# Float32 projections replaced by three float32r products of high and low parts, in the front of an attention and channel-mixing kernel

## The reference

```python
def attn(x):                       # 16 heads of 16 channels
    q, k, v = (heads(x @ W.T + b) for W, b in ((Wq, bq), (Wk, bk), (Wv, bv)))
    attn = softmax(einsum('bhnd,bhmd->bhnm', q, k) * 4.0)
    return concat(einsum('bhnm,bhmd->bhnd', attn, v)) @ Wo.T + bo
def mix(x):
    xr, xk = mu_r * x + (1 - mu_r) * x_prev, mu_k * x + (1 - mu_k) * x_prev
    return sigmoid(xr @ W_r.T) * (relu(xk @ W_k.T) ** 2 @ W_v.T)
x = x + attn(layernorm(x))
x = x + mix(layernorm(x))
```

## Time and profile before

| | us |
|---|---|
| median of three runs | 2742.4 |
| profiled execution | 2745.94 |
| its span, first to last instruction | 2744.2 |
| mean granted TensorE clock (share of full) | 0.999 |
| TensorE, VectorE, ScalarE, GpSimd busy | 2719.2, 2484.4, 2494.8, 373.5 |

### The profile page before, as it was taken

The page is one execution under the profiler, slowest core; times in us unless marked ns, Lnnn a source line. Parts: engine busy times, 40 slices in busy tenths (PEclk is TensorE's granted clock), DMA queues, the critical chain, the costliest instruction groups (busy, mean ns, idle before and its releaser), DMA issues.

```text
span 2744.2 us, 57924 instructions
## 1 busy us (share of the span) xinstructions
PE 2719.2 (99%) x22619; PEld 904.0 (33%) x22619; DVE 2484.4 (91%) x4853; ACT 2494.8 (91%) x2800; POOL 373.5 (14%) x752
## 2 busy tenths in 40 slices
PE   9999999999999999999999999999999999999999
PEld 6552222222222222222222222222222222224776
DVE  6659999999999999999999999999999999985774
ACT  7779999999999999999999999999999999987555
POOL 7761000000000000000000000000000000103451
PEclk9999999999999999999999999999999999999999
DMA  6642010100000000000010101010101000212541
GB/s 198 214 156 59 12 35 12 28 19 21 21 23 24 23 23 24 23 23 24 17 30 10 33 12 34 12 35 12 34 13 45 24 22 20 60 41 79 167 131 47
DMA packets 145363, 126.30 MB, mean 46 GB/s; under 512 B 59969, under 2 KB 127425, under 8 KB 145089
## 3 DMA queue, kind: packets, MB, share of 16 engines
q1 hardware_dynamic: 145088, 122.59, 14.9%
HBM read 72.75 MB, written 47.19 MB: 44 GB/s over the span
## 4 chain that ended last, share of the span: by engine, by line
PE 85%; SPq 9%; DMA 2%; DVE 2%; issue 1%; ACT 1%; POOL 0%; POOLq 0%; ACTq 0%
PE psum L1359 34%; PE psum L1255 17%; PE psum L1327 16%; PE psum L1389 4%; PE psum L1907 3%; SPq L153 3%; SPq L158 3%; PE psum L1270 3%; PE psum L1404 2%; PE psum L447 2%; PE psum L1895 2%; SPq L126 2%; DMA a_qs<-q_parts 2%; SPq L127 2%; DVE a_mx L1033 1%
## 5 line engine op out<-in xcount | busy, mean ns | idle before, releaser
L1033 DVE TENSOR_REDUCE a_mx<-psum 128x1 f32<-128x512 f32 x3096 | 1930.0, 683 | 118.3 <-PE psum L1327 98.9
L1255 PE MATMUL psum<-a_qs,a_ks 50*128 50x512 f16 x4096 | 804.7, 384 | 3.6 <-DMA a_qs<-a_mrows 2.4
L1327 PE MATMUL psum<-a_ks,a_qs 48*128 48x512 f16 x3596 | 759.9, 382 | 12.5 <-DVE a_mx L1033 2.2
L955 ACT ACTIVATE m_gate<-psum 128x1024 f32<-128x1024 f32 x684 | 676.7, 1028 | 29.5 <-PE psum L1255 17.8
L955 ACT ACTIVATE m_y<-psum 128x1024 f32<-128x1024 f32 x682 | 675.0, 1028 | 28.8 <-PE psum L1255 16.9
L955 ACT ACTIVATE p_x<-psum 128x1024 f32<-128x1024 f32 x682 | 674.7, 1028 | 28.9 <-PE psum L1255 17.4
L1255 PEld LDWEIGHTS psum<-a_qs,a_ks 50*128 50x128 f16 x4096 | 193.8, 93 | 677.2 <-ACT m_y L955 166.5
L1359 PE MATMUL psum<-m_gate,a_vst 128*32 128x256 f32 (+1 forms) x4248 | 406.3, 454 | 0.0
L1359 PE MATMUL psum<-p_x,a_vst 128*32 128x256 f32 (+1 forms) x4232 | 403.4, 453 | 0.0
L1359 PE MATMUL psum<-m_y,a_vst 128*32 128x256 f32 (+1 forms) x4224 | 403.2, 453 | 0.0
L1327 PEld LDWEIGHTS psum<-a_ks,a_qs 48*128 48x128 f16 x3596 | 205.7, 93 | 405.9 <-DVE a_mx L1033 328.4
(11 more groups left out here) (147 smaller groups left out, 1605.8 us busy)
## 6 DMA issues: line engine op xcount, KB each, us to landing
m_x<-x SPq DMA_DIRECT2D x24, 512.0 KB, 5.7
a_qs<-q_parts SPq DMA_DIRECT2D x384, 32.0 KB, 2.2
sums<-a_o SPq DMA_DIRECT2D x256, 34.0 KB
q_parts<-m_split SPq DMA_DIRECT2D x16, 512.0 KB, 3.5
v_rows<-m_v SPq DMA_DIRECT2D x16, 512.0 KB, 2.8
k_parts<-m_split SPq DMA_DIRECT2D x16, 512.0 KB, 3.9
a_ks<-k_parts SPq DMA_DIRECT2D x64, 128.0 KB
a_vin<-v_rows SPq DMA_DIRECT2D x64, 128.0 KB, 6.0
```

Source lines behind the costliest of these rows:

```text
L955: ac.activation(p_sb[n % WEIGHTS][:, 2 * pair:2 * pair + 2, :], psum[:, at:at + 2, :], ACT.Exp, scale=SCALE).then_inc(s_exp, 1)
L1033: dve.tensor_reduce(peak, psum[:, bank(at), :], AX.X, ALU.max).then_inc(s_mx, 1)
L1255: mm = te.matmul(psum[:, pair_of_banks(u) + par, :], ks[row:row + MR, (it // QB) % 2, pair, c * P:(c + 1) * P], qs[row:row + MR, it % QRIN ...
L1327: te.matmul(psum[:, bank(slot(n, par)), :], qs[row:row + SR, pit % QRING, at:at + P], keys, start=True, stop=True).then_inc(s_sp, 1)
```

## The change

From block 1 on, q, k and v are computed from parts. ScalarE's copy of the transposed block and of each weight matrix into a float32r tile keeps the high part (`x_high`, `w_high`); VectorE subtracts it from the source to get the low part (`x_low` by `lows`, `w_low` by `weights_low`). Each float32 matmul becomes three float32r matmuls: high by high, low weight by high x, high weight by low x. So a job has six matmuls in place of two, a value half twelve in place of four. Block 0 keeps its float32 matmuls. `turned(blk + 1)` moves ahead of `value(blk, 0)`, and on ScalarE `keep_turned` ahead of `keep_v(blk, 0)`. `turned` waits for `lows` of the block before; `project(blk, 0)` waits for `lows` of its own block ahead of its last two matmuls. `lows(1)` stands before `whole_norm(1)`; `lows(2)`, and each later even one, stands behind the second Newton round; the odd ones stand between two groups of maxima.

The unit rows: GpSimd fills one 32x2048 piece at the start (`set_unit`), and three DMAs on SyncE's queue copy its two rows to the other seven places (`copy_units`, after the loads of x for blocks 2 and 3); the four 32x4096 fills inside the front go, and so does `first_k`'s wait for them.

The attention runs `even(0)`, `odd(1)` first and `sixteen` from period 2 on. The weights' and x parts' tiles are allocated in memory that the last stage's tiles use later. The diff, cut:

```diff
+class FrontBuffers:
+
+
+    def __init__(self, ctx, nc):
+        def sb(name, shape, dt=F32):
+            return ctx.enter_context(nc.sbuf_tensor(name, shape, dt))
+
+        self.w = {n: sb(f"p_w{n}", [P, KH, C]) for n in "qkv"}
+        self.w_high = {n: sb(f"p_wh{n}", [P, KH, C], F32R) for n in "qkv"}
+        self.w_low = {n: sb(f"p_wl{n}", [P, KH, C], F32R) for n in "qkv"}
+        self.w_sq = sb("p_wsq", [P, 2, KH, C])
+        self.x_high, self.x_low = ([sb(f"p_x{n}{s}", [P, KH, TB], F32R) for s in range(2)] for n in "hl")
+
...
-    def set_unit(self, pool, buf, par):
-
-        pool.memset(self.ks[par * HALF + 32:par * HALF + 64, buf, :, :], SHIFT_UNIT).then_inc(self.s_unit, 1)
-        pool.wait_ge(self.s_unit, 2 * buf + par + 1)
+    def set_unit(self, pool):
+
+        pool.memset(self.ks[32:64, 0, 0, :], SHIFT_UNIT).then_inc(self.s_unit, 1)
+
+    UNITS_INC = 3 * DMA
+
+    def copy_units(self, sp):
+
+        sp.wait_ge(self.s_unit, 1)
+        rows = self.ks[SR:MR, 0, 0, :]
+        other = slice(HALF + SR, HALF + MR)
+        sp.dma_start(self.ks[SR:MR, 0, 1, :], rows).then_inc(self.s_units, DMA)
+        sp.dma_start(self.ks[SR:MR, 1, :, :], rows.unsqueeze(1).to_broadcast([PARTS, GP, N])).then_inc(self.s_units, DMA)
+        sp.dma_start(self.ks[other, :, :, :].rearrange("p b u n -> p (b u) n"),
+                     rows.unsqueeze(1).to_broadcast([PARTS, 2 * GP, N])).then_inc(self.s_units, DMA)
 
...
     def first_k(self, sp, n):
-        if n == 0:
-            sp.wait_ge(self.s_unit, 2)
-        else:
+        if n:
             sp.wait_ge(self.s_k, self.K_INC * n)
         self.load_k(sp, n)
...
-    w_sb = {n: sb(f"p_w{n}", [P, KH, C], F32) for n in "qkv"}
+    w_sb, w_high, w_low, w_sq = front.w, front.w_high, front.w_low, front.w_sq
+    x_high, x_low = front.x_high, front.x_low
...
+    low = Steps(sem("p_s_low"), ["low0", "low1"])
...
+        inputs.copy_units(sp)
         next_x(0)
...
-        sp.wait_ge(inputs.s_unit, 4)
+        sp.wait_ge(inputs.s_units, inputs.UNITS_INC)
...
         pool.wait_ge(s_turner, 3)
+        inputs.set_unit(pool)
+        pool.wait_ge(inputs.s_unit, 1)
         pool.memset(v_st[:, :, :, :], 0.0).then_inc(s_one, 1)
         pool.wait_ge(s_one, 1)
...
-            if blk in (1, 2, 5, 6):
-                least.wait(pool, blk, f"part1_kd{KH - 1}")
-                inputs.set_unit(pool, int(blk >= 5), (blk - 1) % 4 % 2)
...
-                act.done(ac.copy(xnT[blk % 2][:, h, :], psum[:, TURNED + h, :]))
+                act.done(ac.copy(x_high[blk % 2][:, h, :], psum[:, TURNED + h, :]))
+
+        def weights_high(n):
+            ac.wait_ge(s_w[n], DMA)
+            ac.copy(w_high[n][:, :, :], w_sb[n][:, :, :]).then_inc(s_wh, 1)
...
             ac.activation(w_sq[:, n, :, :], w_sb["qk"[n]][:, :, :], ACT.Square).then_inc(s_sq, 1)
+        weights_high("q")
         normalise_first()
+        weights_high("k")
         keep_first_turned()
+        weights_high("v")
         ac.wait_ge(s_gain, 13)
         for blk in range(BLOCKS):
             keep_projected(blk)
-            keep_v(blk, 0)
             if blk + 1 < BLOCKS:
                 keep_turned(blk + 1)
-            else:
+            keep_v(blk, 0)
+            if blk + 1 == BLOCKS:
                 exp(0, 0, 0)
                 copy(0)
             if 0 < blk < BLOCKS - 2:
...
+        def weights_low(n, count):
+
+            dve.wait_ge(s_wh, count)
+            dve.tensor_tensor(w_low[n][:, :, :], w_sb[n][:, :, :], w_high[n][:, :, :], ALU.subtract
+                              ).then_inc(s_wl, 1)
+
+        def lows(blk):
+
+            if blk < BLOCKS:
+                for h in range(KH):
+                    act.wait(dve, blk, f"xnT{h}")
+                    low.done(dve.tensor_tensor(x_low[blk % 2][:, h, :], psum[:, TURNED + h, :],
+                                               x_high[blk % 2][:, h, :], ALU.subtract))
...
         bounds()
+        weights_low("q", 1)
         first_turned()
         gains()
         statistics(1)
         whole_norm(0)
         normalised(1)
+        weights_low("k", 2)
+        weights_low("v", 3)
         statistics(2)
         statistics(3)
+        lows(1)
         whole_norm(1)
         normalised(2)
...
             lead(blk, 2)
+            if blk:
+                lows(blk + 1)
             lead(blk, 3)
             if more:
...
                 newton(pair, 1)
+            lows(blk + 2)
             lead(blk + 1, 3)
             if more:
...
         def turned(blk):
 
-            act.wait(te, blk - 1, "xnT1")
+            if blk > 1:
+                low.wait(te, blk - 1, "low1")
...
+            out, s = psum[:, j % 2, :], blk % 2
+            if blk == 0:
+                for k in range(KH):
+                    mm = te.matmul(out, w_sb[n][:, k, h * P:(h + 1) * P], xnT[:, k, :], start=(k == 0),
+                                   stop=(k == KH - 1))
+                pe.done(mm)
+                return
+            if (blk, j) in ((1, 0), (1, 2)):
+                te.wait_ge(s_wl, j // 2 + 1)
             for k in range(KH):
-                mm = te.matmul(psum[:, j % 2, :], w_sb[n][:, k, h * P:(h + 1) * P],
-                               xnT[blk % 2][:, k, :], start=(k == 0), stop=(k == KH - 1))
+                te.matmul(out, w_high[n][:, k, h * P:(h + 1) * P], x_high[s][:, k, :], start=(k == 0), stop=False)
+                te.matmul(out, w_low[n][:, k, h * P:(h + 1) * P], x_high[s][:, k, :], start=False, stop=False)
+            for k in range(KH):
+                if j == 0:
+                    low.wait(te, blk, f"low{k}")
+                mm = te.matmul(out, w_high[n][:, k, h * P:(h + 1) * P], x_low[s][:, k, :], start=False,
+                               stop=(k == KH - 1))
             pe.done(mm)
...
+            if (blk, half) == (1, 0):
+                te.wait_ge(s_wl, 3)
             for t in range(2 * half, 2 * half + 2):
+                out, tokens, s = psum[:, value_at(blk, half), (t % 2) * C:(t % 2 + 1) * C], slice(t * P, (t + 1) * P), blk % 2
                 for k in range(KH):
-                    mm = te.matmul(psum[:, value_at(blk, half), (t % 2) * C:(t % 2 + 1) * C],
-                                   xnT[blk % 2][:, k, t * P:(t + 1) * P], w_sb["v"][:, k, :],
-                                   start=(k == 0), stop=(k == KH - 1))
+                    first, last = k == 0, k == KH - 1
+                    if blk == 0:
+                        mm = te.matmul(out, xnT[:, k, tokens], w_sb["v"][:, k, :], start=first, stop=last)
+                    else:
+                        te.matmul(out, x_high[s][:, k, tokens], w_high["v"][:, k, :], start=first, stop=False)
+                        te.matmul(out, x_high[s][:, k, tokens], w_low["v"][:, k, :], start=False, stop=False)
+                        mm = te.matmul(out, x_low[s][:, k, tokens], w_high["v"][:, k, :], start=False, stop=last)
             pe.done(mm)
...
+        def odd(p):
+
+            f, n, c = FILLS * p, FULL * LEAD + LESS * p, SPAN * p
+            fill(f + 4)
+            peaks(n + 1)
+            times_v(c)
+            fill(f + 5)
...
+            peaks(n + 14)
+            fill(f + 21)
...
             lead(blk, 2)
+            if blk + 1 < BLOCKS:
+                turned(blk + 1)
             value(blk, 0)
             lead(blk, 3)
-            if blk + 1 < BLOCKS:
-                turned(blk + 1)
-            else:
+            if blk + 1 == BLOCKS:
...
-        for p in range(0, PERIODS - LEAD - 1, 2):
+        even(0)
+        odd(1)
+        for p in range(2, PERIODS - LEAD - 1, 2):
             sixteen(p)
         even(PERIODS - LEAD - 1)
...
-        attend_inputs = AttendInputs(ctx, nc, q_d, k_d, kd_d, v_d)
+        with ExitStack() as front_ctx:
+            front = FrontBuffers(front_ctx, nc)
         mix_inputs = MixInputs(ctx, nc, a["x"], sums_d, rden_d, a["bv"], a["woT"], a["bo"], a["fwrT"],
                                a["fwkT"], a["fwvT"], a["mu_r"], a["mu_k"])
+        attend_inputs = AttendInputs(ctx, nc, q_d, k_d, kd_d, v_d)
```

More of the change, by code:

```diff
@@ L16 @@
 F16 = mybir.dt.float16
+F32R = mybir.dt.float32r
 I32 = mybir.dt.int32
@@ L475, in free_ahead, with stage_attend @@
             self.dx.wait(te, 2, "x10")
-def stage_attend(ctx, nc, psum, x, wqT, wkT, wvT, bq, bk, q_d, k_d, kd_d, v_d, sums_d, inputs, ahead):
+def stage_attend(ctx, nc, psum, x, wqT, wkT, wvT, bq, bk, q_d, k_d, kd_d, v_d, sums_d, inputs, ahead, front):
     LEAD = 3
@@ L532, in stage_attend @@
     xn, full, v_sb = ahead.xn, ahead.whole, ahead.v_sb
-    xnT = [t[:, :, 1:TB + 1] for t in ahead.xT]
+    xnT = ahead.xT[0][:, :, 1:TB + 1]
     parts = [t[:, :, :].rearrange("p a n -> p (a n)").bitcast(F16).rearrange("p (j a t) -> p j a t", j=4, a=PARTS)
@@ L541, in stage_attend @@
     s_w = {n: sem(f"p_s_w{n}") for n in "qkvb"}
+    s_wh = sem("p_s_wh")
+    s_wl = sem("p_s_wl")
     s_turner = sem("p_s_id")
@@ L916, in keep_first_turned @@
                 an.done_alone(ac)
```

(5 more changed lines are left out.)

45 lines of the change are left out of this document (42 added, 3 removed).

## The result

The changed kernel takes 2731.06 us (median of 5 runs, 2730.35 to 2731.5), the kernel before 2744.3 beside it: ratio 0.9951, 95% interval 0.9936 to 0.9965. That is faster, as forecast, by 13.2 us where 14.5 were worked out. (2728 was forecast from a kernel before that had run 2742.4; beside the changed one it ran 1.9 longer.)

The account below looks back on a forecast made before the run. TensorE was taken to bound the front, ScalarE 1.6 us per block behind. Terms 7.7 - 5.0 + 1.0 - 9.3 - 4.7 - 2.5 - 1.7 = -14.5 us, on the median 2742.4 giving 2728; range 2719 to 2745.

Parts of the forecast that it names:

- the start: Blocks 1 and 2: VectorE's new work delays the norms and low parts, TensorE idles and its clock halves; +7.7 us.
- blocks 2 to 5: Front blocks: each falls from TensorE's 11.46 us to 10.2, near ScalarE's 9.88 of work; -5.0 us.
- block 15: Last front block and attention entry: maxima-row transfers keep their length, so only the work around them gains; -1.7 us.
- the pairs: Blocks 6 to 11, score tiles and statistics: VectorE becomes the bound, 26.12 to 23.0 us per pair; -9.3 us.
- pair 12-13: Pair without statistics: VectorE light, ScalarE plus waits for tiles gives 21.4 us; -4.7 us.
- block 14: No normalising on ScalarE; TensorE's products, tiles and waits set the length, 12.76 to 10.3 us; -2.5 us.
- One pass: TensorE's projections: a float32r product takes one pass, 0.214 us per 512 columns, against two for float32; 8.7 us per block.
- Rival 1: Value halves: weight loads set the pace, blocks stay at 11.5 us, the start is still lost; 2751 us, chance 0.11.
- The SyncE term: Stores of blocks 3 and 4: 18 us of transfers don't shrink while ScalarE reaches block 6 sooner; +1.0 us.
- Unit rows and GpSimd: Front: GpSimd is no bound, its 14 us of fills worth nothing by themselves; the three replacing DMAs cost 0.
- Order of the first steps, weights' high parts: First 16 attention steps: 0, between -1.5 and +2.2 us; ScalarE's weight copies at the start: 0, or 1.8 without waits.
- Rival 2: VectorE's front: the lock holds `weights_low` (+2.3 us) and pairs stay at 25.5 us; 2737.6 us, chance 0.14.

Follow-up runs that it names:

- run 4: Changed kernel without VectorE forming the low parts of x from block 3 on (stale ones multiplied): 2724.95 us, one execution.
- run 3: Kernel before with only the new unit rows (one early 32x2048 fill, three DMA copies, no fills between blocks): 2744.84 us, ratio 1.000.
- run 2: Changed kernel with GpSimd's four 3.5 us unit-row fills back in blocks 1, 2, 5, 6, without the DMA copies and early fill: 2741.85 us, ratio 0.9989.
- run 1: Changed kernel with the attention's first 16 steps in the order of all later ones: 2731.32 us, ratio 0.9948 to the kernel before.
- run 10: Changed kernel with the loads preparing the last stage moved behind the next step's maxima-row DMAs on SyncE's queue: 2725.06 us, ratio 0.9928.
- run 8: Changed kernel with GpSimd's parts of block 1 held until VectorE has normalised block 2: 2730.0 us.
- runs 6 to 8: Changed kernel, separately: block 2's transposes later and low parts earlier, 2729.49 us; GpSimd held until block 2's normalising at block 0, 2731.36, at block 1, 2730.0.
- run 12: Changed kernel with block 2's transposes and low parts moved (low parts behind blocks 4 and 5's statistics), GpSimd's block 1 parts held, preparing loads later: 2719.44 us.
- run 11: Changed kernel with block 2's transposes later and low parts ahead of block 4's statistics, GpSimd's block 1 parts held, preparing loads later: 2723.05 us, ratio 0.9921.

## Why the prediction was right

The mechanism was right in the main, and so was the size; that the sum came out at exactly the -14.5 us of the spans is luck. Against their terms the start was better by 2.7 us, blocks 2 to 5 by 0.8, block 15 and the entry by 0.9 and the attention and all behind it, that step aside, by 0.7; the pairs were worse by 0.8, pair 12-13 by 1.2, block 14 by 0.9, and the step at 2350 us by 2.2. That is 5.2 us each way. By its steps:
- **One pass.** Right; the pitch is 0.233, 9% over the 0.214 read from the float16 row. TensorE is busy 9.6 us in a plain block where 8.7 were forecast. So TensorE bounds pair 12-13 (busy 22.48 of 22.66), where the prediction had ScalarE and waits at 21.4, and block 14 (10.93 of 11.11): -4.7 and -2.5 became -3.5 and -1.6. That is the term that was mis-sized. Rival 1 decided from 0.144 per 256-column product; it was 0.123.
- **The start.** Mechanism right, place by place: the normalising ended at 35.27 (35.6 forecast), low parts at 41.70 (43.1), the clock halved for the value products behind the idling. +5.0 measured where +7.7 and a lower bound of +5 stood. Of the 2.7 between them 0.3 is the normalising, 1.1 that VectorE took 5.15 us from there to the low parts (6.2 forecast), and the rest the clock. The value products at half of it were over at 40.69, so TensorE reached the products that want the low parts at 41.62; the low parts were ready at 41.10 and 41.70. By the two pitches (24 products of 0.213 us against 0.123) TensorE would have reached them some 2 us earlier at full clock, an estimate, and would then have waited for them. That term was put on the path and lay beside it.
- **Blocks 2 to 5.** ScalarE bounds them, 9.84 against 10.2. Its 9.88 us were no floor: back to back its records overlap, and it is busy 9.43. The SyncE term was put at 1.0; it was 1.6 and took all of block 5's gain.
- **Pairs.** 23.37 against 23.0, so nearly right in size, but "VectorE becomes the bound" holds for the last 0.7 us only (run 4), and it is busy 94% of a pair, not over 95.
- **Unit rows and GpSimd.** The sentence "its 14 us are worth nothing by themselves" is right (run 3) and still misses the point: inside the change they are worth 10.8 us (run 2). The prediction took the fills as gone and so summed correctly, but it did not ask what they would cost in shorter blocks. There they shut out VectorE and, with 8.3 + 3.5 us in a block of 9.84, make GpSimd late. Had the change kept the fills, the forecast would have been 10 us too good.
- **Order of the first steps, weights' high parts.** The order is worth 0, as forecast (run 1). The weights' high parts were not tried by themselves.
- **Not forecast at all:** the step at 2350 us, which gave 2.2 back. It goes with the loads ahead of one transpose on SyncE's queue, since run 10 removes it by moving them. It was 39.71, 41.95, 41.36, 38.99 or 38.47 us long in kernels that don't differ there; what makes it one or the other is open.

Rival 2 (the lock at the front) did not come as priced. The first `weights_low` began 0.17 us before GpSimd's first subtraction, the second followed at once, and neither was held. GpSimd's first four subtractions lasted 5.51 us instead of the 4.59 of later ones. The changed kernel's VectorE and GpSimd:

```profile
19.94 0.69 DVE L1161 TENSOR_TENSOR p_wlk<-p_wk,p_whk 128x512 fp32r<-128x512 f32 x1
20.54 0.69 DVE L1161 TENSOR_TENSOR p_wlv<-p_wv,p_whv 128x512 fp32r<-128x512 f32 x1
20.11 5.51 POOL L872 TENSOR_TENSOR m_split<-m_whole,m_split 128x512 f16<-128x512 f32 x4 [13.52 <-DVE m_xn L1155]
```

GpSimd paid. The same page and section of the Trainium skill says that issue order decides who blocks; the first of these rows agrees, and the second shows that the operation behind it was not held either. The prediction cited this page for `weights_low`, which paid nothing, and passed over the line on tensor_scalar. That line bears on what did cost: the normalising (4.33 us for 1.38) and the fill at the start of run 2.

## What to carry to other kernels

Work on an engine with slack isn't free if it shuts out a neighbour: before calling it hidden, list what the other engine does at that moment and whether somebody waits for it. The price of such a thing changes when another part of the change takes the slack away, so try parts alone and left out, both ways; here 0 and 10.8 us. And time idled away by TensorE can be paid twice, as in run 8, where the products behind it ran at half the clock. Closing one gap (runs 6 to 8) bought 0 to 1.4 us by block 15, closing all of them at once (run 12) 5.8.

## What the runs showed of the hardware

- A fill of 32x4096 on GpSimd (3.50 us) held a 128x8 tensor-with-scalar operation of VectorE for 3.24 us (run 2), and let tensor-with-tensor ones of 0.17 us pass (the kernel before, 37.99 to 39.4 us).
- A 128x8 operation of VectorE, beside GpSimd's 1.16 us subtractions, lasted 1.1 us instead of 0.17, four times in one Newton chain (run 11); four reductions from PSUM kept their 2.47 us beside a fill (run 2, from 103.04).
- float32r products: 0.233 us per 512 columns and 0.123 per 256 at full clock, 0.43 (run 8) and 0.213 (the changed kernel, from 36 us) at half.
- In run 12 TensorE idled 0.4 us of block 1 and 0.6 us of block 2, and the clock never left 1.00; in the changed kernel it idled 1.7 of the 4 us from 32 on, and in the 4 us after that the granted clock was 0.50.
